# Four-layer graph network on one core: rows from HBM, four tiles a round, nothing picked in the second graph convolution

## The reference

```
L0: h = relu(edge_attr @ W1 + b1)                  # 128 hidden
    W = (h @ W2 + b2) as 16 x 16;  m = x[src] @ W   # summed by dst
L1: two graph convolutions (16 -> 32 -> 16):  m = dis[src] * w * dis[dst] * xw[src]
L2: m = h[src] @ rel_weight[type230] + rel_emb[type230], hyperbolic maps before and after
L3: m = h[src] @ basis_weight[type90], scaled by an attention term of both ends and edge_attr
```

## Time and profile before

| | us |
|---|---|
| median of the runs | 28181.01 |
| profiled execution | 28230.68 |
| its span | 28228.9 |
| PE busy | 14862.8 (53%) |
| DVE busy | 10546.7 (37%) |
| ACT busy | 9892.9 (35%) |
| POOL busy | 12908.9 (46%) |
| mean granted TensorE clock | 0.685 of full |

### The profile page before, as it was taken

One profiled execution on the slowest core, in us unless ns is written; L12 is line 12 of the kernel. 1 busy time (PEld: TensorE's weight loads), 2 busy tenths in 40 slices (PEclk: granted clock), 3 DMA queues, 4 the chain that ended last, 5 costly groups with the idle time before them and its releaser, 6 DMA issues.

```text
span 28228.9 us, 246637 instructions
## 1 busy us (share of the span) xinstructions
PE 14862.8 (53%) x73042; PEld 11976.1 (42%) x73042; DVE 10546.7 (37%) x17029; ACT 9892.9 (35%) x17300; POOL 12908.9 (46%) x13642
## 2 busy tenths in 40 slices
PE   4555555554777776777776344444444233333333
PEld 3444444443555554555555333333333223223232
DVE  3333333343222222222222444444444344444444
ACT  2333333333444443444443333333333222222221
POOL 4444444444444444444444444444444455555554
PEclk6777777776888887888888666666666555555555
DMA  1000000000000000000000000000000001000010
GB/s 19 12 13 13 13 13 13 13 13 12 10 11 11 11 11 11 10 11 11 11 11 10 9 9 9 9 9 9 9 9 9 10 15 15 15 15 15 15 15 15
DMA packets 775177, 332.80 MB, mean 12 GB/s; under 512 B 458949, under 2 KB 757528, under 8 KB 774278
## 3 DMA queue, kind: packets, MB, share of 16 engines
q0 software_dynamic: 436000, 115.01, 5.0%
q1 hardware_dynamic: 338534, 210.53, 2.6%
HBM read 161.98 MB, written 162.54 MB: 11 GB/s over the span
## 4 chain that ended last, share of the span: by engine, by line
another core or an unknown queue 35%; PE 28%; issue 11%; DVE 10%; DVEq 7%; ACT 6%; POOL 2%; ACTq 1%; DMA 0%; SPq 0%; POOLq 0%
PE PS L666 13%; DVE big L1102 5%; PE PS L624 4%; PE PS L668 3%; DVEq L1107 3%; PE PS L741 3%; PE PS L608 2%; POOL big L523 2%; DVE acc L1065 1%; DVEq L1069 1%; ACT oneh L865 1%; ACT tabo L775 1%; DVEq L889 1%; ACT big L863 1%
## 5 line engine op out<-in xcount | busy, mean ns | idle before, releaser
L514 POOL DMA_INDIRECT gat<-table,idx x10000 | 9475.7, 948 | 10877.0 <-DMA wgt<-in_edge_weight 3502.0
L1102 DVE TENSOR_TENSOR big<-PS,gat 128x512 f32<-128x512 f32 (+3 forms) x4875 | 3322.6, 682 | 10519.0 <-remote 7890.7
L666 PE MATMUL PS<-tparts,poneh 125*128 125x400 f32 x20000 | 4915.8, 394 | 2015.4 <-issue 1133.8
L666 PEld LDWEIGHTS PS<-tparts,poneh 125*128 125x128 f32 x20000 | 4000.6, 214 | 2458.6 <-issue 1471.8
L514 POOL DMA_INDIRECT gat<-in_x,idx x3125 | 2956.4, 946 | 3836.1 <-DMA att<-in_edge_attr 2921.2
L863 ACT ACTIVATE big<-PS,negrel 128x512 bf16<-128x512 f32 x2625 | 1587.4, 639 | 7965.7 <-remote 5899.3
L741 PE MATMUL PS<-wx,oneh 115*128 115x272 f32 x12500 | 2613.2, 375 | 2413.4 <-DVE big L1102 1947.4
L624 PE MATMUL PS<-w0b_sb,tabo 128*128 128x256 f32 x6250 | 2347.7, 473 | 2855.5 <-issue 1524.3
L1226 DVE TENSOR_REDUCE gat<-PS 128x16 f32<-128x400 f32 x2500 | 1411.1, 574 | 5951.9 <-PE PS L668 2796.7
L741 PEld LDWEIGHTS PS<-wx,oneh 115*128 115x128 f32 x12500 | 2317.2, 263 | 2588.1 <-DVE big L1102 2097.8
L719 PE MATMUL PS<-identb,typb 128*128 128x128 bf16 x6250 | 961.1, 298 | 4393.2 <-ACT oneh L865 3013.2
(11 more groups left out here) (275 smaller groups left out, 12609.9 us busy)
## 6 DMA issues: line engine op xcount, KB each, us to landing
gat<-table,idx POOLq DMA_INDIRECT x10000
running<-msg SPq DMA_DIRECT2D x250, 212.5 KB
gat<-in_x,idx POOLq DMA_INDIRECT x3125
running<-msg SPq DMA_DIRECT2D x250, 200.0 KB
running<-msg SPq DMA_DIRECT2D x125, 400.0 KB
att<-in_edge_attr SPq DMA_DIRECT2D x125, 200.0 KB
idx<-in_src SPq DMA_DIRECT2D x625, 12.5 KB
big<-running,endi POOLq DMA_INDIRECT x500
```

Source lines behind the costliest of these rows:

```text
L514: pool.indirect_dma_start(g[:, j, 0:GW[l]], None, tab_dram[l][:, :], bass.IndirectOffsetOnAxis(ap=idx[:, s, j:j + 1], axis=0)).then_inc(ga ...
L666: pe.matmul(o, poneh[0:NQ, m, c], tparts[0:NQ, k, m * JC:m * JC + JC], start=m == 0 and k == 0, stop=False)
L1102: dve.tensor_tensor(products(j, n), of, xs, ALU.mult).then_inc(mats_free, 1)
```

## The change

- Stage 2 gathers all 25 tiles; nothing is picked (PK[2] = 0). Stage 1 picks as before, but in groups of 4, 4 and 2 tiles: one `picks` signal and one maximum per group.
- What was spread by TensorE comes as rows from HBM. Before stages 1, 3 and 4 the codes or types of all edges are transposed once (`flip`: 25 blocks or fewer through PSUM, ScalarE copies them, SP writes a row per chunk to HBM). Per chunk SP loads that row to all 128 partitions (`spread_rows`, three buffers), and ScalarE makes the distances of the whole chunk at once, the one-hots in halves of 12 and 13 tiles, or per pick group.
- Products go by rounds of four tiles: 7 in stages 3 and 4; in stage 0, 8 groups of tiles k, k+8, k+16 (and 24).
- Stage 0: the hidden layer of a group is one matmul of up to 512 columns; b2 is no longer added per edge: x @ b2 (`k_b2`) stands beside x in a table of 32 columns, is gathered with it and added after the reduction. Both one-hots for counting are built by VectorE, in the fourth round. The attributes of the next chunk are turned late in this one. The first gather now waits for that table.

```
@@
-    SLOTS = [4, 0, 0, 2, 4]
-    PK = [0, 10, 10, 0, 0]
+    SLOTS = [2, 2, 2, 2, 4]
+    PK = [0, 10, 0, 0, 0]
+    GW = [32, 16, 16, 16, 17]
+    HALF = [(0, 12), (12, CH - 12)]
+    PRIOR = [3, 3, 2, 2, 5]
+    GROUPS = [[(slice(k, CH, 8), len(range(k, CH, 8))) for k in range(8)], None, None] + 2 * [[(slice(t, t + n), n) for t, n in QUADS]]
@@ SP
+            def spread_rows(l, it, s):
+                sp.wait_ge(rows_used, it * S + (SPREAD.index(l) * NCH + s + 1 + S - PRIOR[s]))
+                n = NCOL * P if l <= 2 else CH * P
+                of = code_dram if l <= 2 else type_dram[l - 3]
+                sp.dma_start((rows_h if l <= 2 else rows_b)[:, HOME[s], 0:n],
+                             of[bass.ds(it * S + s, 1), :].rearrange("a n -> (a n)").partition_broadcast(P)
+                             ).then_inc(rows_in[s], 16)
@@ PE, stage 0
-                            pe.matmul(o, hsb[:, j % 2, u * P:u * P + P], w0b_sb[:, :], start=True, stop=False)
-                            last = pe.matmul(o, onesb[0:96, :], b0s[0:96, :], start=False, stop=True)
+                        n = P * GROUPS[0][k][1]
+                        pe.matmul(PS[:, 4 + k % 2, 0:n], w0blk[:, k, :], atT[:, 0:n], start=True, stop=True).then_inc(h_psum, 1)
...
+                            last = pe.matmul(PS[:, b, (u % 2) * CC:(u % 2) * CC + CC], hsb[:, k % 2, u * P:u * P + P],
+                                             w0b_sb[:, :], start=True, stop=True)
@@ PE, stages 3 and 4
-                                last = pe.matmul(PS[:, 4, u * P:u * P + P],
-                                                 typb[:, s, t0 + u:t0 + u + 1].to_broadcast([P, P]), identb[:, :],
-                                                 start=True, stop=True)
-                            last.then_inc(tb_psum, 1)
+                            for b, (h0, _) in enumerate(HALF):
+                                if t0 == h0:
+                                    pe.wait_ge(oneh_ready, it * (S * 2) + (o0 + 2 * s + b + 1))
+                            mats_wait(l, c0 + NQD * s, it, i)
@@ ACT, stages 3 and 4
+                for h in range(halves):
+                    last = act.activation(dist[:, h, :], rows_b[:, HOME[s], :], ACT.Abs, bias=negrel[:, h:h + 1])
+                last.then_inc(rows_used, 1)
...
+                for b, (t0, n) in enumerate(HALF):
+                    if b == 1 and l == 3 and not first:
+                        norms(it * S + s)
+                    act.wait_ge(mats, it * (S * NQD) + (o0 + NQD * s - NQD + (3, NQD)[b]))
+                    c = slice(t0 * P, t0 * P + n * P)
+                    act.activation(oneh[:, 0:halves, c], dist[:, 0:halves, c], ACT.Relu,
+                                   bias=ones_col[:, 0:1], scale=-1.0).then_inc(oneh_ready, 1)
@@ DVE
-                for j, (t0, n) in enumerate(PAIRS):
-                    dve.tensor_tensor(products(j, n), of, xs, ALU.mult).then_inc(mats_free, 1)
+                for j, (tiles, n) in enumerate(groups):
+                    dve.tensor_tensor(products(j), matv(l, j, n), xs, ALU.mult).then_inc(mats_free, 1)
@@ DVE, stage 0
+                        if j == 3:
+                            dve.wait_ge(hist_done, it * S + (s + 1))
+                            dve.tensor_tensor(ohq[:, :, :], bc_r(iota_q[:, 0:NQ], CH), bc_c(dq[:, k], NQ), ALU.is_equal)
...
+                    then(dve.tensor_tensor(a[:, :, 0:C], a[:, :, 0:C], gatv(s, 0)[:, :, C:2 * C], ALU.add))
```

More of the change, by code:

```diff
@@ L100, in build_gnn, with mat_base, flip_rounds, flip_base @@
     MAGIC = 1.5 * 2 ** 23
+    def mat_base(l):
+        return sum(NCH * len(GROUPS[k]) for k in MATS if k < l)
+    FLIPS = [1, 3, 4]
+    def flip_rounds(l):
+        cols = NCOL * NCH if l == 1 else TILES
+        blocks = [(P * b, min(P, cols - P * b)) for b in range((cols + P - 1) // P)]
+        return [blocks[r:r + 16] for r in range(0, len(blocks), 16)]
+    def flip_base(l):
+        return sum(len(flip_rounds(k)) for k in FLIPS if k < l)
     def ga_base(l):
@@ L636, in _, with flip @@
             straddle(0)
-            pe.wait_ge(ev["strad_used0"], 1)
+            def flip(l):
+                of, one = (flat_h, identh) if l == 1 else (flat_b, identb)
+                pe.wait_ge(flat_ready, FLIPS.index(l) + 1)
+                for r, blocks in enumerate(flip_rounds(l)):
+                    if r:
+                        pe.wait_ge(flip_sb, flip_base(l) + r)
+                    for b, (c0, n) in enumerate(blocks):
+                        last = pe.matmul(PS[0:n, 4 + b // 4, b % 4 * P:b % 4 * P + P], of[:, c0:c0 + n], one[:, :],
+                                         start=True, stop=True)
+                    last.then_inc(flip_psum, 1)
@@ L664, in pick_pass @@
+                            pe.wait_ge(picks_free, it * (S * NGR) + (NGR * (y * NCH + s) + NGR + back))
+                            for u in range(n):
+                                o = PS[:, 4 * (i % 2) + u, 0:JC]
+                                c = slice((t0 + u) * P, (t0 + u) * P + P)
                                 for m in range(BK):
@@ L667, in pick_pass @@
                                                   start=m == 0 and k == 0, stop=False)
-                                pe.matmul(o, poneh[0:JR, BK, c], rival[0:JR, :], start=False, stop=True
-                                          ).then_inc(picks, 1)
-                            spread((s + 1) % S, i)
+                                last = pe.matmul(o, poneh[0:JR, BK, c], rival[0:JR, :], start=False, stop=True)
+                            last.then_inc(picks, 1)
+            flip(1)
+            pe.wait_ge(ev["strad_used"], 1)
             pick_pass(1)
@@ L793, in root_of, with flip @@
                 act.activation(to, of, ACT.Sqrt).then_inc(ev[done], 1)
+            def flip(l):
+                to = flip_h if l == 1 else flip_b
+                for r, blocks in enumerate(flip_rounds(l)):
+                    act.wait_ge(flip_psum, flip_base(l) + r + 1)
+                    for b in range(0, len(blocks), 4):
+                        c0, n = blocks[b][0], min(4, len(blocks) - b) * P
+                        last = act.copy(to[:, c0:c0 + n], PS[:, 4 + b // 4, 0:n])
+                    last.then_inc(flip_sb, 1)
             root_of("cnt_sqrt_in", na[0:NQ, 1, :], na[0:NQ, 0, :], "cnt_sqrt")
+            flip(1)
             root_of("deg_in", na[0:NQ, 1, :], na[0:NQ, 0, :], "deg_sqrt")
@@ new lines, in pick_digits @@
+                        act.wait_ge(rows_in[s], it * 16 + (16 * IT * SPREAD.index(l) + 16))
+                        code = rows_h[:, HOME[s], :]
+                        for m in range(BK):
+                            act.activation(pdist[:, m, :], code[:, 0:NPK * P], ACT.Abs, bias=negbank[:, m:m + 1])
+                        act.activation(pdist[:, BK, :], code[:, NPK * P:2 * NPK * P], ACT.Abs,
+                                       bias=negbank[:, 0:1]).then_inc(rows_used, 1)
+                        act.drain()
@@ L834, in _ @@
             last.then_inc(ev["c1_relu"], 1)
-            pick_digits(2)
+            with act.Fori(0, IT) as it:
+                for s in range(S):
+                    run_mask(2, it, s)
+                    act.drain()
+            flip(3)
             root_of("ln_in1", na[0:NQ, 3, :], na[0:NQ, 2, :], "ln_out1")
@@ L1351, in _ @@
                     hyper_chunk(it, s, lambda j, s=s: finish(it - (s == 0), (s - 1) % S, j))
[L1352 removed]
+            for j in range(NQD):
                 finish(IT - 1, S - 1, j)
```

447 lines of the change are left out of this document (211 added, 236 removed).

## The result

The changed kernel takes 28,454.21 us (median of 4 runs, 28,446.29 to 28,507.74) beside 28,218.35 for the kernel before on the same chip (4 runs, 28,180.32 to 28,267.56): a ratio of 1.0089, 95% interval 1.0073 to 1.0105. It is slower by 0.9%, little but clear of the noise. Forecast were 24,860 us, with 22,700 to 27,300 as the range.

The account below looks back on a forecast made before the run. TensorE's signals coming late while gathers run were taken to bound most chunks. Stages of 48.4 + 26.3 + 31.4 + 43.3 + 38.2 = 187.6 us a chunk gave 28,231 - 3320 - 50 = 24,860 us, range 22,700 to 27,300.

Parts of the forecast that it names:

- The number of products in a window: Product groups expected to finish while a chunk's gathers run: 2 of 8, 2 of 3, 4 of 7, 5 of 7.
- the signal's price: Under gathers, each TensorE signal costs time whatever its size; as a rival alone 22,830 us, chance 0.22.
- The rival in which a tile has the price: Under gathers, delay goes by tile, so coarser groups only wait longer: 27,430 us, chance 0.20.
- ScalarE is a chunk ahead of VectorE, so I cost it at zero.: SP's added row DMA per chunk, behind a wait for ScalarE's use of a row buffer, costs nothing.
- My ceiling: Most that SP's row DMA could cost if ScalarE fell behind: 4 us a chunk, 1500 us over three stages.
- Stage 2 at 1.25 us a gather: Unpicked stage 2 is bound by 25 gathers at 1.25 us, 31.4 us a chunk with GpSimd's loop.
- Stage 0's one-hots "covered": VectorE's 6.2 us of one-hots after stage 0's fourth product fall in the gather window and add nothing.
- The sum: Five stages at 187.6 us a chunk, 124 intervals: 23,262 us against 26,581, 3320 less.
- the free chunks at the stages' ends: Chunks after a stage's last gather take 28, 21, 26 and 21.6 us in stages 0, 1, 3 and 4.
- the rows' DMA: Loading a chunk's row to 128 partitions, 819 KB, takes 6 us at 134 GB/s, prefetched.
- the rival of a slow broadcast: Reading one HBM line 128 times is slow, 54.6 us a chunk at 15 GB/s: 30,500 us, chance 0.05.
- -50 us outside the chunks: Start of the kernel 50 us shorter, the three transpositions counted as 0.

Follow-up runs that it names:

- early rows: Changed kernel with SP issuing each chunk's row DMA one chunk earlier in stages 1, 3 and 4; prompt 20,087.58 us, ratio 1.0715 to the kernel before.
- Pairs against quads: Changed kernel, rows one chunk earlier, products of two tiles against four; late: stage 3 48.4 against 51.9 us, stage 4 44.2 against 42.4 to 42.6.
- other_transfers_again: Changed kernel, rows one chunk earlier, gathers replaced by memsets (stage 0), SP's (3) and GpSimd's (4) plain DMAs; late 27.3, 29.2, 21.6 us a chunk.

## Why the prediction was wrong

What failed, by its own steps, in the condition it was made in (forecast 187.6 us over the five chunks, measured 217.1):

- **The number of products in a window** (2 of 8, 2 of 3, 4 of 7 and 5 of 7 in stages 0, 1, 3 and 4) cost the most: 3.4, 4.4, 8.6 (of stage 3's 13.6, after 5.0 for the rows) and 4.7 us, at most 21.1 of the 29.5. In the traces above 2 of 7 got through in stage 3 (with late rows), and 7 in a double window in stage 4, 3.5 for one. I took the signal's price mostly as its own. The rival in which a tile has the price gave 50.7, 31.9, 50.8 and 43.5 for stages 0, 1, 3 and 4; measured are 51.8, 30.7, 51.9 (with early rows) and 42.9. Pairs against quads speak for it: the size is worth +3.5 us in one stage and -1.7 in the other. I gave that rival 0.20. Its total, 27,430 us, would still have been 1000 us too low, by the next two points.
- **"ScalarE is a chunk ahead of VectorE, so I cost it at zero."** It is not, in stage 3: SP issues a chunk's rows behind the store of an earlier chunk, and there a chunk counts as done only at the end of the next one's products. Price 5.0 us a chunk in the late condition (620 us), 9.0 in the prompt one. My ceiling was 4 us, the DMA alone; the 5.8 us of distances and 2.8 of one-hots behind it, which I had listed as work, were not on it.
- **Stage 2 at 1.25 us a gather.** Measured 1.39 in the late condition, 34.8 us for 31.4. The gathers themselves were longer, 1.050 us for 0.95. VectorE's work at the chunk's end was shown to lengthen them in the prompt condition, by 0.6 us a chunk; for the rest the cause is open. That GpSimd never sleeps was right, and the prompt condition gave 31.8.
- **Stage 0's one-hots "covered".** They hold the gathers: 3.5 us a chunk by the two gathers above, of which 1.4 were there before. In the late condition 2.7 us went when ScalarE made the larger one, so that of stage 0's 3.4 us in the first point little is left for the window.

The sum has a small slip too: 26,581 us counts 123 intervals of stage 3 and 23,262 counts 124, so the same steps give 24,810 us, not 24,860.

What held: the free chunks at the stages' ends (27.0, 21.5, 29.6 and 21.5 us for 28, 21, 26 and 21.6; stage 3's is longer by its late rows), the rows' DMA (4.3 us, so the rival of a slow broadcast is out), and -50 us outside the chunks (-71).

Behind all this stands what the prediction had not asked: what got through a window depended less on instructions or tiles than on how long gathers had run without a pause, in one condition of the machine. The counts in the earlier trace rows were taken over a run of 31 us that begins free and then gets stuck. In the earlier trace rows the first 6 us of it had been free, and I had read them as an onset to be left out, not as what a shorter run would be like throughout.

## What to carry to other kernels

When an engine's signals are late while another engine works, try a pause in that other engine before making the signals fewer: two drains a chunk took 19% off the kernel before, fewer and larger groups nothing. Before costing a prefetch at zero, walk the issuing queue in order and ask which event each wait ahead of it stands for, above all where a chunk's "done" is deferred. And a change that moves work from one engine to another pays only if it relieves the engine that binds: ten tiles picked by TensorE were cheaper than ten more gathers on GpSimd, by 4.0 us a chunk late and 10.3 prompt.

## What the runs showed of the hardware

- The same kernel and data take 18,750 us in one condition and 28,200 in the other, and a chip can be in either. In the prompt one a semaphore update follows TensorE's matmul by 14 ns; in the late one 1073 of 4875 products start over 1 us after the matmuls that they need, one of them 19.4 us. What sets the condition is open.
- In the late condition delays build up within a run of indirect gathers on GpSimd, spaced 1.25 us. The first 3 to 9 us go by free, depending on the stage, and a pause of 2.7 us lets through what was held. The same number of plain DMAs, from SP or from GpSimd, delays nothing.
- What is still held when the last gather ends comes the later the longer the run was (medians): 1.6 us after 5 gathers and 2.3 after 12 (the versions with drains, stage 3), 4.4 after 25 (kernel before, stage 3) and 7.0 after 50 (changed kernel, stage 0).
- A drain behind a gather holds GpSimd for 1.5 to 1.6 us (prompt), one behind a memset for 0.13 (`other_transfers_again`, stage 0), so a gather's own end at 0.95 us is not the end of GpSimd's work for it.
- A VectorE comparison in bf16 of 2.75 or 3.41 us blocks a gather that starts beside it until 0.81 us after its end (prompt).
